# Typed pass of a graph kernel: the weighting and the node sum move to the head of a turn

## What is computed

```python
W = jnp.einsum('rb,bio->rio', comp, basis)      # a 64x64 matrix for each type
msg = node_feats[src] * norm                    # norm: one weight for each edge
seg = etype.astype(jnp.int32) * N + dst
s = jax.ops.segment_sum(msg, seg, num_segments=R * N).reshape(R, N, -1)
h = jnp.einsum('rni,rio->no', s, W) + bias
```

## Time and profile before

| | us |
|---|---|
| median of three runs | 13067.97 |
| lowest and highest | 13048.71 and 13082.49 |
| the profiled execution, whole | 13061.65 |
| its span in the profile | 13059.6 |
| typed pass in it | about 565 to 5645 |
| granted TensorE clock, mean of the span | 0.754 of full |

### The profile page before, as it was taken

How to read it: one execution, slowest core, us unless ns; L and a number is a source line. 1 busy time by engine, 2 the same in 40 slices (tenths; PEclk the granted TensorE clock), 3 DMA queues, 4 the chain that set the end, 5 groups by cost and what they waited for, 6 DMA issues and landing times. The chain is left out here.

```text
span 13059.6 us, 144784 instructions
## 1 busy us (share of the span) xinstructions
PE 7317.3 (56%) x52908; PEld 5611.8 (43%) x52956; DVE 6785.9 (52%) x8156; ACT 2833.4 (22%) x2654; POOL 6396.0 (49%) x6717
## 2 busy tenths in 40 slices
PE   9755545455555555469999998333333333333334
PEld 4333333333333333359998998222222222222223
DVE  5466666666666666652223223455544555445555
ACT  4333333333333333330000001111111111111112
POOL 4465565665665665610000000666666666666665
PEclk9866666667676766689999999666666666666667
DMA  9733332333332333349997997433333333333332
GB/s 389 307 100 104 104 100 99 109 100 104 105 100 99 109 100 103 106 173 369 371 370 289 370 370 269 97 93 96 91 92 92 93 95 92 92 92 92 95 93 65
DMA packets 480426, 2020.11 MB, mean 155 GB/s; under 512 B 193465, under 2 KB 246136, under 8 KB 354776
## 3 DMA queue, kind: packets, MB, share of 16 engines
q1 hardware_dynamic: 205304, 1283.59, 28.0%
q0 software_dynamic: 206272, 317.25, 10.4%
q10 hardware_dynamic: 68768, 418.23, 8.7%
HBM read 1385.92 MB, written 632.61 MB: 155 GB/s over the span
## 5 line engine op out<-in xcount | busy, mean ns | idle before, releaser
L428 POOL DMA_INDIRECT big<-Yd,ix x3223 | 3049.2, 946 | 2020.8 <-PE ps L535 1046.4
L1303 POOL DMA_INDIRECT big<-Pd,mt x3223 | 3048.9, 946 | 1806.9 <-issue 938.8
L527 PE MATMUL ps<-ring 128*128 128x490 bf16 x3223 | 1423.6, 537 | 2177.0 <-DVE ring L465 979.8
L462 DVE TENSOR_TENSOR ring<-ps,vw 128x2940 bf16<-128x2940 f32 (+1 forms) x516 | 1726.3, 3346 | 1723.3 <-PE ps L529 1305.9
L1332 DVE TENSOR_TENSOR ps<-ps,big 128x1024 f32<-128x1024 f32 x403 | 481.9, 1226 | 2341.4 <-DMA big<-Pd,mt 2341.4
L527 PEld LDWEIGHTS ps<-ring 128*128 128x128 bf16 x3223 | 412.4, 128 | 2971.2 <-issue 2098.1
L1439 PE MATMUL ps<-idt,total 128*128 128x128 f32 x135 | 64.0, 474 | 2459.4 <-issue 2398.4
L535 PE MATMUL ps<-big 128*65 128x128 f32 x6446 | 1135.3, 347 | 355.1 <-issue 354.3
L535 PEld LDWEIGHTS ps<-big 128*65 128x65 f32 x6446 | 1050.0, 186 | 444.9 <-issue 442.3
L549 ACT ACTIVATE Z<-ps 128x1470 bf16<-128x1470 f32 (+1 forms) x584 | 799.0, 1399 | 1780.0 <-remote 913.8
L549 ACT ACTIVATE big<-ps 128x1470 bf16<-128x1470 f32 (+1 forms) x576 | 787.2, 1398 | 1719.4 <-remote 924.1
(11 more groups left out here) (215 smaller groups left out, 11658.7 us busy)
## 6 DMA issues: line engine op xcount, KB each, us to landing
Yd<-big SPq DMA_DIRECT2D x196, 1024.0 KB, 8.8
Aj<-Z SPq DMA_DIRECT2D x65, 3062.5 KB
big<-Aj SPq DMA_DIRECT2D x130, 1531.2 KB, 8.4
cb<-Aj ACTq DMA_DIRECT2D x130, 1531.2 KB, 8.4
Aj<-big SPq DMA_DIRECT2D x64, 3062.5 KB
cb<-Aj SPq DMA_DIRECT2D x128, 1531.2 KB, 8.4
Z<-Aj ACTq DMA_DIRECT2D x128, 1531.2 KB, 8.5
dr<-in_dstr SPq DMA_DIRECT2D x135, 1152.0 KB
```

The lines of the kernel that those rows point to most:

```text
L428: e.indirect_dma_start(gv[j][:, k, 0:64], None, table, bass.IndirectOffsetOnAxis(ap=ix[j][:, k:k + 1], axis=0)).then_inc(sm[f"g{j}"], 16)
L462: nc.vector.tensor_tensor(one[r][:, 0:m, :], bc_t(iof, m, W * NT), bc_f(vw[j][:, k], m, W * NT), ALU.is_equal)
L527: nc.tensor.matmul(PS[q][:, 0:W * NT], olo[r][:, c, :], one[r][:, c, :], start=True, stop=False)
L1303: e.indirect_dma_start(gv[j][:, k, :], None, Pd, bass.IndirectOffsetOnAxis(ap=mt[j][:, k:k + 1], axis=0)).then_inc(sm[f"g{j}"], 16)
```

## The change

Reordering within a turn; no operation is added but one wait and one increment on POOL.

- POOL: within the 25 gathers of block b, the fifth one waits until the node sum of block b-1 is done.
- DVE: a turn begins with the weighting of block b's rows, then the indices of block **b+2** (which wait for the load of block b+2), then groups 0 to 3 in a row. Behind them come the other tables of block b+2 (`prep`, `weight`) and the target table of block b+1 (`targets`), and `add` of block b's own sum. The tables of blocks 0 and 1 are made ahead of the loop.
- PE: the node sum of block b comes first in the turn, ahead of the block's adjacency matmuls.
- SP and ACT are unchanged.

```diff
@@ gpsimd
-                    for k in range(LA if at(b, NA - 1) else KA):
+                    first, last, n = at(b, 0), at(b, NA - 1), reg(e, b + 1)
+                    for k in range(LA if last else KA):
+                        if k == 4 and not first:
+                            e.wait_ge(sm["pe"], n)
+                            e.sem_inc(sm["pool"], 1)
                         e.indirect_dma_start(
@@ vector
-                def prep(b, j, loaded, n):
+                def indices(j, loaded):
                     e.wait_ge(sm[f"m{j}"], loaded)
                     nc.vector.scalar_tensor_tensor(out=ix[j][:, :], in0=mt[j][:, 0:KA], scalar=float(NR),
                                                    in1=mt[j][:, KA:2 * KA], op0=ALU.mult, op1=ALU.add).then_inc(sm["ix"], 1)
+
+                def prep(j, n):
@@
+                def targets(j, n, kn):
+                    e.wait_ge(sm["pe"], n)
+                    nc.vector.tensor_tensor(oh[:, 0:kn, :], bc_t(iof[:, 0:P], kn, P), bc_f(rl[j][:, 0:kn], kn, P), ALU.is_equal)
+
                 def turn(b, j, i):
@@
+                    e.wait_ge(sm[f"g{j}"], 16 * KA * i + 16 * kn)
+                    nc.vector.tensor_tensor(gv[j][:, 0:kn, 0:64], gv[j][:, 0:kn, 0:64], bc_f(pw[j][:, 0:kn], kn, 64),
+                                            ALU.mult).then_inc(sm["mul"], 1)
+                    if more:
+                        indices(j, 16 * i + 32)
                     if not first:
                         e.wait_ge(sm["cm0"], c0)
                     e.wait_ge(sm["vw"], n)
                     group(j, 0, n)
-                    if not first:
-                        e.wait_ge(sm["mul"], b)
-                    if not last:
-                        prep(b + 1, 1 - j, 16 * (i + 1 + j), reg(e, b + 2))
                     e.wait_ge(sm["cm0"], c1)
                     group(j, 1, n)
-                    e.wait_ge(sm["pe"], n)
-                    nc.vector.tensor_tensor(oh[:, 0:kn, :], bc_t(iof[:, 0:P], kn, P), bc_f(rl[j][:, 0:kn], kn, P), ALU.is_equal)
                     e.wait_ge(sm["cm2"], c1)
                     group(j, 2, n)
-                    if not first:
-                        add(b - 1, 1 - j)
-                    if not last:
-                        weight(1 - j)
                     e.wait_ge(sm["cm1"], c2)
                     group(j, 3, n)
-                    e.wait_ge(sm[f"g{j}"], 16 * KA * i + 16 * kn)
-                    nc.vector.tensor_tensor(gv[j][:, 0:kn, 0:64], gv[j][:, 0:kn, 0:64], bc_f(pw[j][:, 0:kn], kn, 64),
-                                            ALU.mult).then_inc(sm["mul"], 1)
+                    if more:
+                        e.wait_ge(sm["gb3"], n)
+                        prep(j, reg(e, b + 3))
+                    if not last:
+                        targets(1 - j, reg(e, b + 2), nxt)
+                        add(b, j)
+                    if more:
+                        weight(j)
@@ tensor
                 def turn(b, j, i):
+                    e.wait_ge(sm["mul"], n)
+                    kn = LA if last else KA
+                    for k in range(kn):
+                        mm = nc.tensor.matmul(ag[j], gv[j][:, k, :], oh[:, k, :], start=(k == 0), stop=(k == kn - 1))
+                    mm.then_inc(sm["pe"], 1)
                     for k in range(LA if last else KA):
                         ...
-                    e.wait_ge(sm["mul"], n)
-                    kn = LA if last else KA
-                    for k in range(kn):
-                        mm = nc.tensor.matmul(ag[j], gv[j][:, k, :], oh[:, k, :], start=(k == 0), stop=(k == kn - 1))
-                    mm.then_inc(sm["pe"], 1)
```

More of the change, by code:

```diff
@@ L474, in weight @@
                     nc.vector.tensor_copy(pw[j], wgt_[j]).then_inc(sm["pw"], 1)
+                def targets(j, n, kn):
+                    e.wait_ge(sm["pe"], n)
+                    nc.vector.tensor_tensor(oh[:, 0:kn, :], bc_t(iof[:, 0:P], kn, P), bc_f(rl[j][:, 0:kn], kn, P), ALU.is_equal)
                 def turn(b, j, i):
-                    first, last, b = at(b, 0), at(b, NA - 1), reg(e, b)
+                    first, last, more = at(b, 0), at(b, NA - 1), type(b) is not int or b + 2 < NA
+                    nxt = LA if at(b, NA - 2) else KA
+                    b = reg(e, b)
                     n, c0, c1, c2 = reg(e, b + 1), reg(e, 3 * b), reg(e, 3 * b + 1), reg(e, 3 * b + 2)
                     kn = LA if last else KA
+                    e.wait_ge(sm[f"g{j}"], 16 * KA * i + 16 * kn)
[3 more added lines that the diff above has]
+                        indices(j, 16 * i + 32)
                     if not first:
@@ L483, in turn @@
                     group(j, 0, n)
-                    if not first:
-                        e.wait_ge(sm["mul"], b)
-                    if not last:
-                        prep(b + 1, 1 - j, 16 * (i + 1 + j), reg(e, b + 2))
                     e.wait_ge(sm["cm0"], c1)
                     group(j, 1, n)
-                    e.wait_ge(sm["pe"], n)
-                    nc.vector.tensor_tensor(oh[:, 0:kn, :], bc_t(iof[:, 0:P], kn, P), bc_f(rl[j][:, 0:kn], kn, P), ALU.is_equal)
                     e.wait_ge(sm["cm2"], c1)
                     group(j, 2, n)
-                    if not first:
-                        add(b - 1, 1 - j)
-                    if not last:
-                        weight(1 - j)
                     e.wait_ge(sm["cm1"], c2)
                     group(j, 3, n)
-                    e.wait_ge(sm[f"g{j}"], 16 * KA * i + 16 * kn)
-                    nc.vector.tensor_tensor(gv[j][:, 0:kn, 0:64], gv[j][:, 0:kn, 0:64], bc_f(pw[j][:, 0:kn], kn, 64),
-                                            ALU.mult).then_inc(sm["mul"], 1)
-                e.wait_ge(sm["io"], 8)
-                prep(0, 0, 16, 1)
-                weight(0)
+                    if more:
[6 more added lines that the diff above has]
+                        weight(j)
+                e.wait_ge(sm["io"], 8)
+                for j in range(2):
+                    indices(j, 16)
+                    prep(j, j + 1)
+                    weight(j)
+                targets(0, 1, KA)
                 short_blocks(e, turn, NA)
```

## The result

The changed kernel takes **14084.59 us** (median of four runs, 14068.07 to 14113.62); the kernel before, in the same series, 13068.14 (13048.71 to 13082.49). The ratio is 1.0782, with a 95% interval of 1.0768 to 1.0796: slower by 1016 us. The forecast was 13690 with a range of 13150 to 14100: the right side, and the right wait as the cause, but 395 us too little. The time lies 15 us inside the range's upper end.

What follows compares the result with a forecast made beforehand. POOL's gathers and its wait for a node sum delayed by held PE increments bound the kernel, 39.17 us a turn. Two turns become 88.3 us, 5.0 more per turn, 126 times: 13061.65 + 630 = about 13690 us, range 13150 to 14100.

Steps and rivals of the forecast that it cites:

- two-turn loop: Typed pass: held pieces, store, load, groups, weighting and sum close over two turns, 88.3 us; chance 0.78.
- The deciding step: DVE's indices, before group 0, wait for block b+2's load, issued behind block b-1's store; some 15 us each turn.
- The queue behind the store: SP's queue: the load's packets come after the 3.1 MB store's, so 9.2 us from store to loaded.
- The time of the last release: PE's held increments come out 3.7 us after the last gather, 34.7 us after POOL's fifth gather.
- the hold: PE's increments held from about 20 us into a run of gathers until some 3.7 us after its end.
- my own sign: Forecast is wrong if ACT copies pieces 7 and 8 within 6 us of group 3.
- A term was taken as nothing: DVE to PE: the node sum can begin as soon as the weighting ends, 0 us between.
- The ends of the pass: First turn's later groups, last block's sum and two last turns without a load: counted together as zero.
- The premise: Typed pass: an unbroken run of gathers delays PE's increments from about 20 us in until after its end.
- Rival A: The hold does not reach the pieces; loop closes within one turn, 38.7 us, 13000 to 13150 us; chance 0.12.
- Rival B: Load lands before the weighting is done, POOL's loop sets the turn: 37.8 us, -170, 12890 us; chance 0.08.
- Rival C: POOL reaches its fifth gather with the sum long done, so gathers never pause; over +2500 us; chance 0.02.

Runs made afterwards that it cites:

- second group: Four follow-up runs, the unchanged kernels and two variants without POOL's wait, on a chip where the kernel before took 13062.87 us.
- e7_late_again: Changed kernel with block b+2's indices made behind group 3 instead of before group 0, where increments are held: 12855.99 us, 0.9827 of the kernel before.
- e6: Changed kernel with the indices made behind group 3 and POOL's fifth-gather wait removed: 15102.46 us, 1.1561 of the kernel before.
- e8: Kernel before with the 14th gather waiting for group 3 of the block before, where increments are held: 13064.31 us, ratio 0.9986.
- e5_no_pool_wait: Changed kernel without POOL's wait at the fifth gather, where increments are held: 14308.63 us, 1.0953 of the kernel before.
- e1: Changed kernel with the indices made behind group 3, where increments are not held: 13326.92 us, 1.1363 of the kernel before.

## Why the forecast was right, and where it was off

The two-turn loop, each term as a mean over the turns of the changed kernel (counted from POOL's fifth gather):

| term | forecast | measured |
|---|---|---|
| fifth gather to the store's issue | 37.8 | 40.3 |
| store's issue to the indices' end | 9.3 | 9.3 |
| four groups | 26.4 | 29.3 |
| group 3's end to the weighting's end | 6.8 | 6.2 |
| weighting's end to the sum | 0 | 1.4 |
| the sum | 7 | 7.1 |
| POOL's restart | 1.0 | 0.8 |
| two turns | 88.3 | 94.4 |

Two turns of 47.2 us are 94.4: the seven terms of the loop are the whole of two turns. Against the forecast it is 6.1 us more in two turns, 3.0 x 126 = about 380 of the 395 us. That the time still fell into the range owes something to luck: on the second group's chip the same kernel took 14170.40 us, above it.

- **The deciding step was right:** the indices wait for a load behind the store, 11.5 us a turn, and that wait closes the loop over two turns. e7_late_again shows it from the other side: without it 37.8 us instead of 47 to 48.
- **The queue behind the store was right:** the indices start 9.1 us after its issue, and the earlier trace rows gave 9.2.
- **The time of the last release was right, what waits for it was not.** Pieces 5 and 6 are seen 34.8 us after the fifth gather (2052.11 - 2017.33) against 34.7. But I had group 3 built before the hold, with pieces 7 and 8 of it waiting. In fact group 3 itself stands at the hold's edge: it starts 10.67 us after group 2 where the others take 6.55, so 4.1 us late where I had taken 1.5 out of 0 to 5. This is the term that was sized worst. Then pieces 7 and 8 are not held but not yet computed: PE takes up the last chunks only when ACT has copied the released pieces, and the store leaves 5.5 us after the release, not 3.1. By my own sign (pieces 7 and 8 copied within 6 us of group 3) the trace is on the edge: ACT begins at 5.5 us and ends at 7.6 (it begins at 5.5 in the median of the turns, from 3.2 to 11.5).
- **A term was taken as nothing:** the weighting's end no longer starts the sum, for in many turns PE has the late chunks ahead of it: 1.4 us in the mean, up to 5.8, and 0.06 in the median.
- The ends of the pass and the other stages cost nothing, as taken.
- **The premise was off, in its end and in its start.** Over turns 1 to 126 I took each piece for which ACT stood idle, and call it late when ACT starts more than 1.2 us after PE took up its last matmul.
  - *The end:* increments are delayed, not shut off until the run is over. In the kernel before, piece 6 is late in 116 turns but always seen inside the run, 3.5 us late in the median; only piece 7 waits for the end, in all 126, and comes 3.0 to 3.9 us behind the last gather. Even my own rows had it: piece 6 is copied at 2039.77 and the first block's piece 5 at 601.23, with gathers until 2045.83 and 627.66. In the changed kernel piece 4 is late in 119 turns, 111 times inside the run, 4.7 us in the median. That is the 4.1 us of group 3.
  - *The start:* in the changed kernel piece 3 is late from 14.3 us into a run, while piece 2 is on time up to 20.8 us.
  - *A count of PE's work fits better, but not well.* I counted matmuls and weight loads taken up since the run began. In the kernel before, pieces are on time at 41 to 49, late in 9 turns at 53 to 61, and nearly always late at 65 to 73. In e7_late_again they are on time in 120 of 126 turns at 69 and always late at 81. In the changed kernel they are on time at 36, late in 40 turns at 48 and in 119 at 60. In e6 and e8 the late piece stands right behind the node sum's hundred, at 116 to 133. No run varied that number alone, so it stays open.
- **Rival A** (the hold doesn't reach the pieces, about 38.7 us) was not seen. **Rival B** (37.8) is what e7_late_again does, by keeping the load out of the path rather than by an early landing. **Rival C** (POOL's wait does nothing) falls with the turn shown, where POOL stands 14.82 us at its fifth gather. e5_no_pool_wait adds that the wait saves 0.8 us a turn.

Is there a better kernel? Where increments are held, e7_late_again: 0.983 of the time. Where they are not, the kernel before (1.136 for the same kernel). No kernel of these beats it on both.

## What to carry to other kernels

When a step is moved forward in an engine's order, ask what feeds it and in which queue that stands: here a 63 KB load stood behind 3.1 MB of store. Before, DVE used a load that had been issued a turn earlier; asking in the same turn for the indices of block b+2 instead of b+1 made a hidden 9 us the longest wait of the loop. A loop that closes over two turns must be summed over two; a term that looks fixed (the store's issue) is itself moved by the delay it causes. And a transfer's time depends on what large transfer it falls beside, so ask of every gain when the next store will start.

## What the chip showed that I had not expected

- **Chips of one type differ by 11% on the same kernel.** The kernel before took 11723 and 11728 us on two chips and 13063 to 13077 on the others. In the typed pass I found one thing in which the traces differ: on the slower ones, increments of PE arrive late while POOL issues gathers (21 us after the matmuls were taken up in the turn of e6_late_no_wait), the last of them 2.4 to 4.5 us after a run's end in the turns shown; on the faster ones they are never late. Why a chip is of one kind or the other, no run shows.
- **Small gathers starve beside a large store on another queue:** 64 packets in 8 us instead of 218, and a gather lands 7.4 us after its issue instead of 1.5.
- **The hold can help.** It delays the store past the last gather, so that e1's kernel is at 37.8 us a turn with it and at 43.6 without.
- **A wait on POOL can pay for itself** where increments are held: POOL's pause lets the node sum and the first pieces through (e5 and e6 without it: 48.9 and 55.1 us a turn, with it 48.1 and, e7, 37.8).
